# Expert tiles inside the mixer's macros, rows scattered into expert order, and another order of work

## Time and profile before

| | |
|---|---|
| median of 3 runs | 1167.79 us (1166.45 to 1168.86) |
| the profiled execution | 1168.7 us |
| its span, first to last instruction | 1166.9 us |
| mean granted TensorE clock | 0.953 |
| busy: PE, DVE, ACT, POOL | 90%, 86%, 73%, 28% |
| PE weight loads busy | 71% |
| DMA, mean over the span | 159 GB/s |
| 4 chain that ended last | DVE 53%, issue 15%, PE 7% |

### The profile page before, as it was taken

How to read it: one execution, slowest core, us unless ns; L and a number is a source line. 1 busy time by engine, 2 the same in 40 slices (tenths; PEclk the granted TensorE clock), 3 DMA queues, 4 the chain that set the end, 5 groups by cost and what they waited for, 6 DMA issues and landing times.

```text
span 1166.9 us, 25635 instructions
## 1 busy us (share of the span) xinstructions
PE 1047.6 (90%) x8826; PEld 823.5 (71%) x8826; DVE 1009.0 (86%) x1837; ACT 850.0 (73%) x1549; POOL 328.4 (28%) x353
## 2 busy tenths in 40 slices
PE   4862599667999999999999999999999999999896
PEld 2532477445888887877877788787788788788675
DVE  5849633349999999999999999999999999999962
ACT  3941222059888888888888888888888888888750
POOL 1305777101222222222222222222222222222230
PEclk9985699977999999999999999999999999999998
DMA  7968366424455544445454555454454444554440
GB/s 232 318 229 354 109 213 211 128 71 128 134 152 155 155 147 149 149 144 161 149 154 148 151 155 154 147 154 147 153 157 154 148 148 146 157 147 152 131 150 21
DMA packets 141014, 185.64 MB, mean 159 GB/s; under 512 B 19950, under 2 KB 101151, under 8 KB 139472
## 3 DMA queue, kind: packets, MB, share of 16 engines
q1 hardware_dynamic: 114608, 146.70, 37.0%
q0 software_dynamic: 15744, 26.23, 11.1%
q10 hardware_dynamic: 10528, 11.01, 2.8%
HBM read 75.99 MB, written 40.63 MB: 100 GB/s over the span
## 4 chain that ended last, share of the span: by engine, by line
DVE 53%; issue 15%; PE 7%; DMA 1%; ACT 1%; DVEq 1%; POOL 0%; SPq 0%; POOLq 0%; ACTq 0%
DVE conv L1156 14%; DVE att L1242 4%; DVE g L1260 3%; DVE decay L1189 3%; DVE prod L1215 3%; DVE prod L1214 3%; PE ps L821 3%; DVE prod L1225 3%; DVE prod L1224 3%; DVE o_tile L1275 2%; DVE phase L1181 2%; DVE state L1250 2%; DVE lam L1173 2%; DVE cown L1229 2%; DVE theta L1164 2%
## 5 line engine op out<-in xcount | busy, mean ns | idle before, releaser
L821 PE MATMUL ps<-xn_in,win 128*128 128x256 f32 x1152 | 292.0, 396 | 25.7 <-DMA xn_in<-xnT_d 15.5
L821 PEld LDWEIGHTS ps<-xn_in,win 128*128 128x128 f32 x1152 | 215.6, 196 | 57.2 <-issue 13.2
L1156 DVE SCALAR_TENSOR_TENSOR conv<-x_pre,col,conv 128x256 f32<-128x256 f32 x480 | 195.1, 477 | 17.4 <-ACT conv L988 17.4
L1313 POOL TENSOR_TENSOR state_in<-state,cin_s 128x256 f32<-128x256 f32 x56 | 45.0, 803 | 387.8 <-DVE state L1250 387.8
L946 PE MATMUL ps<-wout,g 128*128 128x256 f32 x512 | 125.8, 390 | 5.3 <-DVE o_tile L1275 4.6
L946 PEld LDWEIGHTS ps<-wout,g 128*128 128x128 f32 x512 | 96.2, 193 | 22.3 <-issue 9.0
L1332 POOL TENSOR_TENSOR rms<-ms,cst 128x1 f32<-128x1 f32 x64 | 46.8, 732 | 219.0 <-DVE ms L1267 219.0
L933 PEld LDWEIGHTS ps<-att,x_tok 128*64 128x64 f32 x1024 | 54.6, 136 | 49.6 <-issue 28.8
L642 DVE TENSOR_TENSOR r_tiles<-ps,r_expw 128x256 f32<-128x256 f32 x72 | 30.6, 424 | 63.7 <-issue 48.7
L988 ACT ACTIVATE conv<-ps,col 128x256 f32<-128x256 f32 x160 | 83.6, 571 | 0.0
L1242 DVE TENSOR_TENSOR att<-ps,cst 128x1024 f32<-128x1024 f32 x64 | 77.1, 1204 | 5.5 <-PE ps L906 5.5
(11 more groups left out here) (169 smaller groups left out, 2367.7 us busy)
## 6 DMA issues: line engine op xcount, KB each, us to landing
cin_s<-cin SPq DMA_DIRECT2D x128, 129.0 KB, 2.3
rep<-bc_d SPq DMA_DIRECT2D x128, 128.0 KB
grow_s<-grow SPq DMA_DIRECT2D x128, 128.0 KB, 2.1
bup_s<-bup SPq DMA_DIRECT2D x128, 128.0 KB, 2.0
cown_s<-cown SPq DMA_DIRECT2D x128, 128.0 KB, 2.6
expert_d<-r_tiles ACTq DMA_DIRECT2D x18, 512.0 KB, 3.4
xn_d<-r_tokens SPq DMA_DIRECT2D x16, 512.0 KB, 4.3
xnT_d<-r_turned SPq DMA_DIRECT2D x4, 2048.0 KB, 24.1
```

The lines of the kernel that those rows point to most:

```text
L821: last = nc.tensor.matmul(dst, win[:, kt, n * P:(n + 1) * P], xn_in[b][:, kt, :], start=(kt == 0), stop=(kt == KT - 1))
L1156: nc.vector.scalar_tensor_tensor(conv[:, ct, :], x_pre[b][:, ct, tap:tap + MT], c("conv_w", ct * D_CONV + tap), conv[:, ct, :], ALU.mult, ...
```

## The change

- Routing. The one-hot product and `token_of` are gone. The rows are scattered instead: `xs_d` holds xn in expert order. SP first writes zeros to the last tile of each expert and the unused tiles (16 transfers of 128 KB to computed addresses); after them POOL scatters the last 16 tiles, which still lie in SBUF (`kept_sorted`). `xnT_d` is stored from ACT's queue. The steps of dt are interleaved with those of the routing. The expert block is gone.
- The other 48 tiles are scattered by POOL at the head of the mixer, from loads that SP issues in 11 parts (`SORT`): four at the head, three at the end of iteration -2, four at the end of iteration -1. They use `spare`, a new 10 KB a partition, and the two buffers of `att`.
- Expert tiles. 72 tiles, four per iteration in iterations 1 to 18 (part of tile 0 of each four already in the iteration before, on SP). For each: SP loads the rows (128 KB) and the expert's weights with its bias (384 KB), PE turns (2 instructions), ACT copies, PE multiplies (4 instructions), DVE adds, SP stores (128 KB). Their PSUM is the free half of the bank of `back_update`, and PE waits for that bank's other readers.
- Output. Macros before DIRECT = 21 load x alone (`load_x`) and are stored without their expert part; for macros 21 to 31 the gather, scale and add of x stay. The 42 tiles of the first 21 macros are gathered, scaled and added to the output in DRAM by POOL and ACT, four per iteration, from iteration 20 on (`late_gather`, `late_scale`, `late_add`).
- Smaller parts. `xbc` has three buffers instead of one; `x_skip` and its product with the identity on PE (L928) are gone, ACT writes x times D straight into the PSUM bank of y (`back_seed`, 8 instructions of 128x128 a macro); `back_ms` moves from DVE to ACT.
- The order of work of all five lists is new: macro m's scores of ch 1 stand at the head of PE's list, and `front_cin`, `front_waves` and the last third of the convolution come one iteration earlier by their index.

The diff, cut to what decides (indentation reduced by eight):

```diff
+SORT, _row = [], 0
+for _n in range(10):
+    SORT.append((_n % 4, _row, (5, 5, 4, 4)[_n % 4]))
+    _row += SORT[-1][2]
+SORT.append((0, _row, TILES - KEPT * GROUP - _row))
...
+            for n in range(2 * EXPERTS):
+                to = sp.value_load(empties[0:1, n:n + 1], min_val=0, max_val=ASIDE + EXPERTS - 1)
+                sp.dma_start(xs_d.rearrange("(n p) d -> p n d", p=P)[:, bass.ds(to, 1), :], zero_rows[:, None, :]).then_inc(sp_stored, 16)
+            sp.wait_ge(sp_stored, 16 * 2 * EXPERTS)
...
+            pool.wait_ge(sp_stored, 16 * 2 * EXPERTS)
+            pool.wait_ge(rv, ROUTED)
+            for t in range(TILES - KEPT * GROUP, TILES):
+                rows_of = a_xn[(t // GROUP) % AHEAD][:, t % GROUP, :]
+                pool.indirect_dma_start(xs_d, bass.IndirectOffsetOnAxis(ap=slot_of[:, t:t + 1], axis=0), rows_of, None).then_inc(kept_sorted, 16)
+            pool.wait_ge(kept_sorted, 16 * KEPT * GROUP)
...
+def sort_load(sp, n, rows_of):
+    b, at, w = SORT[n]
+    after(sp, sort_done[b], 16 * sort_before(n))
+    sp.dma_start(rows_of[b][:, 0:w, :], xn_d[at * P:(at + w) * P, :].rearrange("(t p) d -> p t d", p=P)).then_inc(sort_loaded[b], 16)
+
+def sort_rows(pool, n, rows_of):
+    b, at, w = SORT[n]
+    pool.wait_ge(sort_loaded[b], 16 * (sum(1 for i, _, _ in SORT[:n] if i == b) + 1))
+    for i in range(w):
+        pool.indirect_dma_start(xs_d, bass.IndirectOffsetOnAxis(ap=slot_of[:, at + i:at + i + 1], axis=0), rows_of[b][:, i, :], None).then_inc(sort_done[b], 16)
...
+def tile_load(sp, j, e_in, e_w):
+    b = j % 2
+    if j == 0:
+        for n in range(4):
+            sp.wait_ge(sort_done[n], 16 * sort_count(n))
+    after(sp, tile_turned, j)
+    sp.dma_start(e_in, xs_d[j * P:(j + 1) * P, :]).then_inc(tile_loaded, 16)
+    e = sp.value_load(tile_expert[0:1, j:j + 1], min_val=0, max_val=EXPERTS - 1)
+    after(sp, tile_added, j - 1)
+    sp.dma_start(e_w[b].rearrange("p k d -> p (k d)"), w_tile[:, bass.ds(e, 1), :].rearrange("p o d -> p (o d)")).then_inc(tile_weights[b], 16)
...
+def tile_turn(pe, j, e_in, e_ps):
+    pe.wait_ge(tile_loaded, 16 * (j + 1))
+    after(pe, tile_added, j)
...
+    PER, FIRST, LATE = 4, 2, 4
...
+    DIRECT = FIRST + SLOT_TILES // PER + 1
+    e_ps = bank_u[:, PAIRS * HEADDIM:]
...
+            j = PER * (m - FIRST) + i
+            if m >= FIRST and j < SLOT_TILES:
...
         sp.wait_ge(m_ready, 3)
+        for n in range(4):
+            sort_load(sp, n, rows_of)
         for m in range(-BEFORE, MACROS):
+            expert_store(m, 3)
+            bounce(m + 2)
+            load_hidden(m + 3)
             load_xn(m + 3)
-            stack_grow(m + 1)
-            load_hidden(m + 3)
+            expert_load(m + 1, 1)
             load_dt(m + 3)
             stack_cin(m + 1)
+            expert_load(m + 1, 2)
             stack_bup(m + 1)
             stack_cown(m + 1)
-            bounce(m + 2)
+            expert_store(m + 1, 0)
+            expert_load(m + 1, 3)
+            load_x(m + 1, 0)
             store(m, 0)
             replicate(m + 2)
+            expert_load(m + 2, 0)
+            expert_store(m + 1, 1)
+            expert_store(m + 1, 2)
+            stack_grow(m + 2)
+            load_x(m + 1, 1)
             store(m, 1)
+            for n in {-2: range(4, 7), -1: range(7, len(SORT))}.get(m, ()):
+                sort_load(sp, n, rows_of)
         for ch in range(TPM):
...
+        def back_update(m, ch, turned, multiplied):
             b, t = m % 2, m * TPM + ch
+            after(pe, tile_evac, tiles_by(m, turned))
+            after(pe, tile_added, tiles_by(m, multiplied))
...
+        nc.tensor.matmul(bank_y, ident, cst[:, 0:PAIRS * P], start=True, stop=True).then_inc(s["opened"], 1)
         for m in range(-BEFORE, MACROS):
-            back_update(m, 0)
             back_scores(m, 1)
+            expert_turn(m + 1, 0, -2)
+            back_out(m, 0)
+            back_update(m, 0, 5, 4)
+            back_turn(m, 1)
+            front_x_a(m + 3)
+            expert_product(m + 1, 0, -1)
+            front_x_b(m + 3)
+            expert_turn(m + 1, 1, -1)
+            front_x_c(m + 3)
+            back_square_sum(m, 0)
             front_turn(m + 1, 0)
-            front_x_a(m + 3)
+            front_theta(m + 3)
+            expert_product(m + 1, 1, -1)
             front_turn(m + 1, 1)
-            front_x_b(m + 3)
-            back_out(m, 0)
             back_y(m, 1)
-            back_square_sum(m, 0)
-            front_x_c(m + 3)
-            back_update(m, 1)
-            front_theta(m + 3)
+            back_update(m, 1, 6, 6)
+            front_z_a(m + 2)
+            expert_turn(m + 1, 2, 0)
+            front_z_b(m + 2)
+            expert_product(m + 1, 2, 0)
+            back_scores(m + 1, 0)
             back_turn(m + 1, 0)
             back_out(m, 1)
-            front_z_a(m + 2)
+            expert_turn(m + 1, 3, 0)
             back_square_sum(m, 1)
-            back_scores(m + 1, 0)
-            front_z_b(m + 2)
             back_y(m + 1, 0)
-            back_turn(m + 1, 1)
+            expert_product(m + 1, 3, 0)
...
+        def back_seed(m, ch):
...
+            after(act, s["gated"], t)
+                last = nc.scalar.activation(bank_y[:, q * P:(q + 1) * P], xbc[m % XBC_BUFS][:, q, ch * P:(ch + 1) * P], ACT.Copy, scale=c("D", q))
...
         act.wait_ge(m_ready, 3)
         for m in range(-BEFORE, MACROS):
-            front_trig(m + 1)
-            front_lambda(m + 2)
-            front_z(m + 1, 0)
-            front_z(m + 1, 1)
+            expert_evacuate(m + 1, 0)
+            front_bpart(m + 1, 1)
             front_round(m + 2)
+            back_square(m, 0)
             back_b(m, 1)
-            front_bpart(m + 1, 0)
-            front_bpart(m + 1, 1)
             front_halo(m + 3)
+            front_x_a(m + 3)
+            back_seed(m, 1)
+            front_x_b(m + 3)
+            expert_evacuate(m + 1, 1)
             front_tok(m + 1, 0)
-            back_scale(m + 1, 0)
+            back_ms(m, 0)
+            front_x_c(m + 3)
             back_scale(m + 1, 1)
-            back_square(m, 0)
+            late_scale(m - 1)
             front_tok(m + 1, 1)
-            front_silu(m + 2)
-            front_x_a(m + 3)
-            front_x_b(m + 3)
-            front_skip(m + 2)
-            front_x_c(m + 3)
+            front_trig(m + 2)
+            front_exp(m + 2)
+            expert_evacuate(m + 1, 2)
+            front_z(m + 2, 0)
+            front_lambda(m + 3)
             back_square(m, 1)
-            front_exp(m + 2)
+            back_seed(m + 1, 0)
+            back_scale(m + 2, 0)
+            expert_evacuate(m + 1, 3)
+            back_ms(m, 1)
             back_b(m + 1, 0)
+            front_bpart(m + 2, 0)
+            front_z(m + 2, 1)
+            front_silu(m + 3)
...
         dve.wait_ge(m_zero, 1)
         for m in range(-BEFORE, MACROS):
-            front_waves(m + 1)
-            front_lamdt(m + 2)
-            front_cin(m + 1)
-            back_gate(m, 0)
-            front_conv(m + 2, range(10, 15))
             back_state(m, 0)
             back_mask(m, 1)
-            front_decay(m + 2)
+            front_lamdt(m + 2)
+            expert_bias(m + 1, 0)
             front_bup(m + 1)
             front_cown(m + 1)
-            back_ms(m, 0)
+            front_frac(m + 2)
+            expert_bias(m + 1, 1)
+            front_clip(m + 3)
+            front_decay(m + 2)
+            back_state(m, 1)
             back_gate(m, 1)
-            front_frac(m + 2)
+            front_phase(m + 3)
             back_final(m, 0)
             front_conv(m + 3, range(0, 10))
-            front_clip(m + 3)
-            back_state(m, 1)
-            back_ms(m, 1)
-            front_phase(m + 3)
             back_mask(m + 1, 0)
+            expert_bias(m + 1, 2)
+            front_waves(m + 2)
             back_final(m, 1)
+            front_conv(m + 3, range(10, 15))
+            expert_bias(m + 1, 3)
+            back_gate(m + 1, 0)
+            front_cin(m + 2)

...
         pool.wait_ge(m_ready, 3)
+        for n in range(len(SORT)):
+            sort_rows(pool, n, rows_of)
         for m in range(-BEFORE, MACROS):
-            back_gather(m + 1, 0)
             back_gather(m + 1, 1)
             back_state(m, 0)
+            back_add_x(m, 0)
             back_rms(m, 0)
-            back_add_x(m + 1, 0)
+            back_state(m, 1)
+            back_gather(m + 2, 0)
+            late_gather(m)
+            back_rms(m, 1)
             back_add_x(m + 1, 1)
-            back_state(m, 1)
-            back_rms(m, 1)
+            late_add(m - 1)
+        pool.wait_ge(late_added, 16 * TPM * DIRECT)
```

639 lines of the change are left out of this document (368 added, 271 removed).

## The result

The changed kernel takes 1290.18 us (median, 1287.97 to 1292.6), the kernel before beside it 1168.32: a ratio of 1.1046 [1.1025, 1.1067], slower by 10%. 1212 was predicted, 1135 to 1245 as the range.

What follows compares the result with a forecast made beforehand. The prediction took DVE, with PE nearly full, to bound the kernel before, and loops through xn the changed one. Start 133, fill 118.5, intervals 887 and tail 77 make 1215.5; adjusted to 1212 us, range 1135 to 1245.

Steps and rivals of the forecast that it cites:

- The loop through xn: Steady iteration: xn landing, PE, DVE, SiLU, bounce and the next xn load close a ring, 30.4 us plain, 32.4 with experts.
- 29.5 apart or less the loop is wrong: Sign for the steady part: clips at most 29.5 us apart would refute the loop through xn.
- The second loop: Steady iteration: expert load waits for tile 3's turn on PE, with later SP loads behind it; nearly the same length.
- Expert intervals: Mixer's 18 iterations with expert tiles: 32.4 us each, bounds 31.1 and 34.5; PE's own work 29.2.
- PE's room: Kernel before, steady iteration: PE has some 0.8 us free of 27.5, read from block starts around theta.
- Rival 1: Steady part: loops don't bind, PE's and DVE's work sets 29.4 and 27.4 us intervals, 1132 us in all; chance 0.22.
- Late intervals: Intervals with late tiles, after the expert stretch: counted among the ten plain ones, 30.4 us each.
- Tail: Last clip to the end: 77 us against 81, with fronts 6 less and late adds some 2 behind the last store.
- Start: Routing to the mixer's start: zero transfers, 16 scatters, block change; about 133 us instead of 232.3, bounds 121 and 140.
- Fill: Mixer's start to the clip of macro 3: 19 + 24 + 29.5 + 46 = 118.5 us, against 83 before.
- step (c): Fill, end of iteration -1: SP stands still until POOL has scattered parts 7 and 8; 46 us for that interval.
- Rival 3: Steady part: transfers get slower, landing 5.9 us, loops 34.5 and 32.2 us, 1282 us in all; chance 0.12.

Runs made afterwards that it cites:

- x1: Changed kernel with the load of xn for the next macro but one moved ahead of bounce in SP's list: 1226.78 us, 1.0484 of the kernel before.
- x4: Changed kernel without expert tiles, the gathers of their rows and the late part; routing and scatter stay: 1188.21 us, 1.0169 of the kernel before.
- x5: Changed kernel without expert tiles, gathers and late part, with the load of xn moved ahead as in x1: 1138.16 us, 0.961 of the kernel before.
- x2: Changed kernel with rms of ch 1 and the add of x ahead of the late gathers on POOL: 1274.76 us, 1.0916 of the kernel before.
- x12: x11 with the loads of parts 10 and 11 behind replicate and the load of xn, and POOL's late adds later: 1170.56, 1167.58 and 1170.75 us.
- x3: Changed kernel with the sort's loads of parts 4 to 10 at earlier iteration ends on SP: 1278.87 us, 1.0929 of the kernel before.
- x6: Changed kernel with the edits of x1, x2 and x3 together: 1206.22 us, 1.0183 of the kernel before.
- x8_all: Changed kernel with all 64 tiles scattered in the mixer, zeros shared by SP and POOL, plus edits of x1 and x2: 1202.48 us, 1.0143 of before.
- b3_block: Kernel before with one more block after the mixer, in which every engine jumps past a single instruction: 1169.45 us, 1.001 of the kernel before.
- b1_before_xn_behind: Kernel before with the load of xn behind bounce on SP, and one PE turn moved ahead for it: 1731.49 us, 1.4811 of the kernel before.
- x11: x8_all with att's buffers only for the first eight sort parts, the last six loads moved, steep-decay experts inside the mixer's block: 1179.12 and 1182.12 us.
- b0_before: Kernel before, unchanged, run again for its trace: 1168.11 us, 0.9998 of the kernel before.

## Why the prediction was wrong

*The loop through xn: right.* x1, x4 and x5 show it; opening it gives back 63 of the 213 us lost in the mixer, more than any other single edit. Its terms, as x4 measured them, are above. By my own sign ("29.5 apart or less the loop is wrong") the plain intervals, 29.5, lie on the border; it is x4 and x5, 29.6 closed and 28.3 open, that decide. In the plain turn (29.5 against 30.4) the landing was the term most off: 3.3 us from xn's issue to the product, against the 4.1 of the earlier trace rows; the earlier trace rows, the short end, was the better row. The 2.6 estimated from "DMA: Bandwidth & Descriptors", "Anatomy of one DMA — SWDGE (gpsimd) path", of the Trainium skill remains below both. The second loop, through the first expert load, is not what holds the expert intervals: with the first open and the second untouched, PE is full in them.

*Expert intervals (32.4, were 33.1).* Within the bounds. PE's work in them was mis-sized, 29.2 for what measures 30.7 in x1's window. In x1_xn_ahead, timeline:

```profile
821.89 1.13 PE L655 MATMUL ps<-spare 128*128 128x256 f32 x4
822.96 1.16 PE L959 MATMUL ps<-cown_s,grow_s 64*128 64x128 f32 x16
...
834.24 1.13 PE L910 MATMUL ps<-hidden,wl2s 49*128 49x256 f32 x4
835.30 0.66 PE L935 MATMUL ps<-cst,xbc 128*128 128x128 f32 x4
```

From start to start this expert product takes 1.07 us and theta 1.06; I had priced both at 0.86, the pace inside a long run. The 0.8 us that I took as PE's room were a reading of the same kind: of the 1.63 us behind theta's start in the earlier trace rows, the bracket gives 0.51 as idle, and theta itself takes the rest. With these rows PE's work would have been 27.5 - 0.5 - 1.9 + 4 x (1.07 + 0.25) = 30.4. PE's wait for xn was smaller for it, 1.6 us an iteration (14.3 in nine, 400 to 700) instead of 3. Rival 1 priced the interval at 29.4 and would have missed by as much.

*Late intervals (30.4, were 33.5): the step that failed.* "18 carry experts", and the other ten were all taken as plain. The late gathers appear in my text only at the end of the tail. I never asked what four more gathers do to the 0.6 us of rms behind them in POOL's queue, and that rms, through DVE's final and the convolution's last third, is a link of the very loop that I had found. The step set this wait at nothing: measured, it is 2.7 us in each of the eight intervals. x2 gives back 1.8 of the 3.1 us; with the loop open, x12's move of the adds another 0.8. 25 us.

*Tail (77, was 100): failed too.* x4_plain, with no late part, has 93.4, of which 79.0 are before DVE's last instruction (before: 73.0) and 14.4 behind it (7.9). So the new order makes the drain 6 us longer, where I had expected 6 less from it; the late part adds 2.7 before DVE's last instruction and 3.9 behind it (18.3 behind it in all; "2 us" in my text); and 6.5 are the skipped block, which I hadn't seen in the diff at all. 23 us. Of the 6 us of the drain 5.3 are DVE's work, by its groups from the last clip to its last instruction, the kernel before (1086 to 1159) and x4_plain (1092.58 to 1171.6):

```profile
L1156 DVE SCALAR_TENSOR_TENSOR conv<-x_pre,col,conv 128x256 f32<-128x256 f32 x6 | 2.5, 475 | 0.0
```
```profile
L1258 DVE SCALAR_TENSOR_TENSOR conv<-x_pre,col,conv 128x256 f32<-128x256 f32 x15 | 6.1, 477 | 0.0
```

In all DVE has 52.2 us of work there, against 46.9 before. The idle time is nearly the same, 27 and 26. The clip, my border, now stands ahead of all 15 steps of the convolution; ten of them used to be in front of it (the sixth of the first row only runs over the window's edge). I took "the 4 of convolution that now come after the clip" off the fill and never added them to the tail. Without the late intervals and the tail the time would have been some 1242, just inside the range.

*Start (133, was 139.3).* SP's zero transfers take 1.42 us each, not 0.85, so POOL starts at 114.75 instead of 107; its scatters keep their pace, 1.27.

```profile
90.34 22.77 SPq L410 DMA_DIRECT2D xs_d<-r_tiles  x16
114.75 1.24 POOL L594 DMA_INDIRECT xs_d<-r_tokens,slot_of  x1 [50.99 <-DMA xs_d<-r_tiles]
```

*Fill (118.5, was 124.4).* 20.4, 23.4, 32.0 and 48.6 for the 19, 24, 29.5 and 46 of the prediction; step (c) was right, as x3 shows. What I took off at the end, 4 us because "every uncertain choice in the fill went the long way", had no row behind it, and went the wrong way: every part but the two plain intervals came out longer.

*The rivals.* Rival 3 came nearest in time (1282) but for a wrong reason: landings were shorter than assumed, not longer.

## What to carry to other kernels

When an order of work is written out by hand, find for each load the last thing that its issuing queue waits for ahead of it, and follow that back to the load's own consumer: if the ring closes within one iteration and is longer than any engine's work, its length is the iteration, whatever the engines' shares say. One line's place cost 63 us here. Do the same for every small operation that a new batch of transfers is put in front of: its queue's time counts, not its own. Price a block of matmuls from where it stands between others, not from a long run of its kind. A change that fills freed time with work in another's queue moves waits along (mask, SP, rep, gather); each mend shows the next, so price them by a trace of each state, not by their sum (1182 by the sum, 1206 measured, in x6).

## What the runs showed of the hardware that was not expected

- A transfer to an address from a register takes SP 1.42 us per issue (16 in 22.8), against 0.34 to 0.59 for fixed ones; where SP and POOL shared them, in x8_all, SP took 1.76 (8 in 14.07) and POOL's came 1.75 to 2.5 us apart.
- POOL's indirect transfers are steady at 0.96 + 0.30 us, but single ones take far longer: 3.7 us once in each of nine late iterations of the changed kernel (1197.61 above), up to 5.7 in x8_all's fill. Dense transfers are not the reason in the late stretch: the DMA share in those nine is 0.14 to 0.29, and 0.75 in a gather of 1.16 us (1194.19). All nine overlap DVE's products of two tiles (epos, wave, grow); no run here tells whether that is the cause. In x2, with rms ahead, the longest late gather is 2.3 us.
- A long block that is only walked past costs 6 us at the end of the program; an empty one 1.1 (b3_block).
- After an idle of 14.5 us PE's clock stood at 0.50 and its first 16 matmuls took 6.7 us, in b1_before_xn_behind.
- The kernel before took 1168 to 1169 us in some sets of runs and 1182 to 1186 in others, 1.2 to 1.5% more, each set steady within 0.3%, on chips of the same numbers (8 and 12) in both sorts. x11, the one new kernel that was measured in both sorts, shows no such step (1179.1 and 1182.1). The one further trace of the kernel before, b0_before, fell among the first sort, so where it loses the 14 us is open.
